# Latent attention: value products of four heads issued as one quad on four column groups, with eight exponential buffers

## The chip, the cores and the metric

One core of a Trainium2 chip runs the whole program. Times are microseconds on the device. The kernel before took 2137.08 us, the median of three runs (2136.1 to 2139.33). Less is better.

## The reference, cut to what matters

The program computes six stages on a state of 16 elements of 256 rows by 128: two mixtures of experts with a gated attention unit between them, a second kind of mixture (gate/up, "swiglu"), a latent attention, and that second mixture again. Only the latent attention changes. For each of the 16 elements (`b`) it computes, with 16 heads of 8 columns:

```python
ct_q = x @ Wd_q_w + Wd_q_b
query = heads(ct_q @ Wu_q_w + Wu_q_b) + heads(_rope(ct_q @ Wq_r_w + Wq_r_b, cos, sin))
ct_kv = x @ Wd_kv_w + Wd_kv_b
key = heads(ct_kv @ Wu_k_w + Wu_k_b) + heads(_rope(x @ Wk_r_w + Wk_r_b, cos, sin))
value = heads(ct_kv @ Wu_v_w + Wu_v_b)
attn = softmax(einsum('bhqd,bhkd->bhqk', query, key) / scale)
out = einsum('bhqk,bhkd->bhqd', attn, value)          # back to (b, s, d_model)
x = x + (out @ Wo_w + Wo_b)
```

All of it is float32. The softmax's maximum of each row is found first (the "search"), then folded into the scores as two extra rows, and its sum comes out of the value product as one more column of ones.

## The kernel before, in words

Each engine has its own program, written out by hand, and the engines wait for each other by counting semaphores (`p.at_ex` counts exponentials, `p.at_av` value products, and so on). The order is a software pipeline over elements: while element b goes through its 16 heads, TensorE also does the end of element b-1 and the preparation of b+1 and b+2 between the heads.

TensorE's order is `at_pe_element` (L1687 on). In step h it issues the scores of head h (`at_scores_pe`, L1644: two matmuls of 26 rows by 128 columns over 256 columns, into bank 3 or 4 in turn, waiting for the exponential of head h-2), and the value products of head h-2 (`at_values_pe`, L1656). Other work hangs on certain steps: 1 the turn of the second half of the maxima's rows (L1606); 2 the turn of the output of b-1 (L1668); 3 the turn of the keys of b+1 (L1582, waits for VectorE's and ScalarE's parts); 4 the turn of x of b+2 (L145); 5 the turn of the queries (L1582); 6 the turn back of the output (L1675); 7 the latent product (L1555); 8 the output product (L1683); 9 the rotary keys (L1563); 7 to 14 two searches each (L1631: 24 rows); 12 the first half of the maxima's rows; 17 the projections of b+2 (L1573, waits for all 16 maxima). Steps 16 and 17 have no scores, only values.

A value product of one head is two matmuls (one for each half of the keys) of 128 rows by 32 columns over 256 columns, accumulated in bank 7. The 32 columns of head a are those from 32 x (a mod 4), so four consecutive heads use four different groups of columns of the array. In the trace each such float32 matmul is two records, so a head is four.

ScalarE's order is `at_act_element` (L1813 on): the exponential of head h (L1818) from bank 3 or 4 into one of four buffers (head mod 4), after the value product of head h-4 has been done; between them copies out of the banks: maxima rows (L1798), parts (L1776), keys and queries (L1781), x, latent, rotary keys (L1756, L1762, L1768), the outputs of heads 0 to 7 after head 9 and of 8 to 15 at the end (L1805).

VectorE's order is `at_dve_element` (L1957 on): the split parts of b+1 (L1897, L1901), the normalised x of b+2 (L136), the norm of the output of b-1 (L1937, L1941), bias and statistics (L1947, L100, L104), two maxima (L1910), the addition to X (L1954), fourteen maxima with two small row writes after the eighth and the sixteenth (L1919, L1921), and the projections' biases and rotation (L1875 to L1888). A search goes into one of three banks, and TensorE waits for the maximum of the search three before it.

The stage's tiles lie in tensors that earlier stages are done with. `g2b` and `be2b` hold the norm weights of the first kind of mixture and are read only there.

Of the kernel before, what the change touches and what calls it, by code (L numbers as in the profile page):

```python
# [13 lines left out]
ACT = mybir.ActivationFunctionType  # L14
AX = mybir.AxisListType

P = 128
B, S, D = 16, 256, 128
# [69 lines left out]
def flat(ap):  # L88
    return ap.rearrange("p a b -> p (a b)")
# [1104 lines left out]
NB2 = 2  # L1194
# [338 lines left out]
NH, HD = 16, 8  # L1533
HR = 32
HQ = P // HR
NHQ = NH // HQ
NPROD = 3 * HD
LATENT = 64
ATT_SCALE = 1.0 / float(np.sqrt(NH + 2 * LATENT))
SEARCH_BANKS = (1, 2, 5)  # L1540
HALF_BANKS = (6, 0)
OUT_BANKS = (5, 6)
LAG = 2
# [23 lines left out]
def at_project_pe(pe, p, b):  # L1567

    pe.wait_ge(p.at_mx.sem, p.at_mx.at(NH * b))
    for n in range(2):  # L1570
        r = slice(n * LATENT, (n + 1) * LATENT)
        for t in range(NB2):
# [48 lines left out]
def at_search_pe(pe, p, b, par, f):  # L1621
# [6 lines left out]
    for n in range(2):  # L1628
        h = pair % HQ + HQ * (2 * (pair // HQ) + n)
        r = head_rows(h, NPROD)  # L1630
        ins = pe.matmul(p.bk[SEARCH_BANKS[f % 3]][:, n * S:(n + 1) * S], p.at_qT[r, h // HQ, t * P:(t + 1) * P],  # L1631
# [4 lines left out]
def at_scores_pe(pe, p, b, par, h):  # L1636
# [3 lines left out]
    if h >= 2:  # L1640
        pe.wait_ge(p.at_ex.sem, p.at_ex.at(NH * b + h - 1))
    r = head_rows(h, NPROD + 2)
    for t in range(NB2):
# [2 lines left out]
    ins.then_inc(p.at_s2.sem, 1)  # L1646


def at_values_pe(pe, p, b, par, a):

    pe.wait_ge(p.at_ex.sem, p.at_ex.at(NH * b + a + 1))
    if a % 8 == 0:
        pe.wait_ge(p.at_op.sem, p.at_op.at(2 * b + a // 8))
    o = p.bk[7][HR * (a % HQ):HR * (a % HQ + 1), (a // HQ) % 2 * S:((a // HQ) % 2 + 1) * S]
    for t in range(NB2):
        ins = pe.matmul(o, p.at_v[:, par, t, a, :], p.at_e[:, a % 4, t * S:(t + 1) * S],  # L1656
                        start=(t == 0), stop=(t == NB2 - 1))
    ins.then_inc(p.at_av.sem, 1)


# [26 lines left out]
def at_pe_element(pe, p, b, par, behind=True, ahead=2):  # L1687


    for h in range(NH + LAG):  # L1690
        if h < NH:
            at_scores_pe(pe, p, b, par, h)
        if h >= LAG:
            at_values_pe(pe, p, b, par, h - LAG)
        if h == 1:
            pe.wait_ge(p.at_kr.sem, p.at_kr.at(b + min(ahead, 1) + 1))
            at_maxima_rows_pe(pe, p, b, 1)
        if behind:
            if h == 2:
                at_out_turn_pe(pe, p, b - 1)  # L1700
            elif h == 6:
                at_out_back_pe(pe, p, b - 1)
            elif h == 8:
                at_out_pe(pe, p, b - 1)
        if ahead >= 1:
            if h == 3:
                at_keys_pe(pe, p, b + 1)
            elif h == 5:
                at_queries_pe(pe, p, b + 1)
            if 7 <= h < NH - 1:  # L1710
                for f in range(2 * (h - 7), 2 * (h - 6)):
                    at_search_pe(pe, p, b + 1, 1 - par, f)
            if h == 12:
                at_maxima_rows_pe(pe, p, b + 1, 0)
        if ahead >= 2:
            if h == 4:
                pe.wait_ge(p.at_q2.sem, p.at_q2.at(2 * b + 2))
                at_x_pe(pe, p, b + 2)
            elif h == 7:
                at_latent_pe(pe, p, b + 2)  # L1720
            elif h == 9:
                at_kr_pe(pe, p, b + 2)
            elif h == NH + LAG - 1:
                at_project_pe(pe, p, b + 2)
# [76 lines left out]

def at_heads_out_act(act, p, b, half):

    act.wait_ge(p.at_av.sem, p.at_av.at(NH * b + 8 * half + 8))
    act.activation(flat(p.at_o[:, 2 * half:2 * half + 2, :]), p.bk[7][:], ACT.Copy).then_inc(p.at_op.sem, 1)  # L1805


# [5 lines left out]
def at_act_element(act, p, b, par, behind=True, ahead=2):  # L1813
    for h in range(NH):
        act.wait_ge(p.at_s2.sem, p.at_s2.at(NH * b + h + 1))
        if h >= 4:
            act.wait_ge(p.at_av.sem, p.at_av.at(NH * b + h - 3))
        act.activation(p.at_e[:, h % 4, :], p.bk[3 + h % 2][:], ACT.Exp, scale=ATT_SCALE).then_inc(p.at_ex.sem, 1)  # L1818
        if h == 1:
            at_maxima_rows_act(act, p, b, 1)  # L1820
        if h == 7 + LAG:
            at_heads_out_act(act, p, b, 0)
        if ahead >= 1:
            if h == 2:
                at_parts_act(act, p, b + 1)
            elif h == 4:
                at_keys_act(act, p, b + 1, 1 - par)
            elif h == 6:
                at_queries_act(act, p, b + 1)
            elif h == 12:  # L1830
                at_maxima_rows_act(act, p, b + 1, 0)
        if ahead >= 2:
            if h == 5:
                at_x_act(act, p, b + 2)
            elif h == 8:
                at_latent_act(act, p, b + 2)
            elif h == 10:
                at_kr_act(act, p, b + 2)
        if behind and h == 7:
            at_out_act(act, p, b - 1)  # L1840
    at_heads_out_act(act, p, b, 1)
# [73 lines left out]
def at_maxima_rows_dve(dve, p, b, half):  # L1915

    h = slice(half * NH // 2, (half + 1) * NH // 2)
    dve.wait_ge(p.at_mx.sem, p.at_mx.at(NH * b + (half + 1) * NH // 2))
    dve.tensor_copy(p.at_sk_r[:, 0, :, h, NPROD], p.at_m[:, :, h]).then_inc(p.at_nm.sem, 1)  # L1919
    dve.wait_ge(p.at_nm.sem, p.at_nm.at(4 * b + 2 * half + 1))  # L1920
    dve.tensor_tensor(p.at_sk_r[:, 0, :, h, NPROD + 1], p.at_m[:, :, h], p.at_sk[:, 0, :, h, NPROD], ALU.subtract)\  # L1921
       .then_inc(p.at_nm.sem, 1)
# [78 lines left out]
def at_pool(pool, p):  # L2001
# [3 lines left out]
    pool.wait_ge(p.at_init.sem, p.at_init.at(2))  # L2005
    pool.memset(p.at_sk[:, 1, :, :, NPROD:NPROD + 2], 1.0).then_inc(p.at_init.sem, 1)
    for par in range(2):
# [5 lines left out]
def at_weights_dve(dve, p):  # L2013
# [25 lines left out]
    "mla": dict(ln_free=B, ln_stat=2 * NT, ln_rs=2 * B, xt=B, at_xc=B, at_ctp=B, at_ct=B, at_krp=B, at_kr=B,  # L2039
                at_prp=2 * B, at_q=NS1 * B, at_hc=2 * B, at_ktp=2 * B, at_kt=2 * B, at_qtp=2 * B, at_qt=2 * B,  # L2040
                at_s1=NH * B, at_mx=NH * B, at_nm=4 * B, at_q2p=2 * B, at_q2=2 * B, at_s2=NH * B, at_ex=NH * B,
                at_av=NH * B, at_op=2 * B, at_otp=B, at_on=4 * B, at_tp=B, at_ot=B, at_wp=B, at_x1=B, at_x=B,
                at_init=5),
    "swiglu": dict(_PREP, **_COMB, gt_rows=NCH * NG, up_rows=NCH * NG, silu_d=NCH * NG, hid_d=NCH * NG, exp_d=E1 * NG,
                   exp_add=TG * E1 * NG, rtg=NG, rt3=2 * NG),
# [62 lines left out]
def work_space(t):  # L2108

    at = Space(t.tables)  # L2110
    w = {n: at.take(P, cols) for n, cols in TABLES.items()}
    at = Space(t.sb_)
    w.update(r=at.take(P, TG, F), rT=at.take(P, 2, F), y=at.take(P, 2, TG, D))
    at = Space(t.sc)
    w.update(yo=at.take(P, 2, TG, D), slots=at.take(P, 2, TG, D), t_ge=at.take(P, SLOT_TILES, E),
             t_skip=at.take(P, SLOT_TILES, E), c_move=at.take(P, TOP * NT, E), xT=flat(t.xf[:]), be1s=t.wd[:, 0:F], w1_last=t.sb_[0:1, :],
             c2s=t.sc[:].rearrange("p (e f) -> p e f", f=F)[:, :, 0:D],
             ga_taken=(flat(t.xf[:]), t.sel[:].rearrange("p k t e -> p (k t e)")))
    at = Space(t.sb_, 2 * W)
    w.update(sw_taken=(at.take(P, W), at.take(P, W)))  # L2120

    w.update(hT=Space(t.sc).take(P, HRING, W), sg=Space(t.sb_).take(P, 2, W))

    at = Space(t.sb_)
    w.update(ga_xa=at.take(P, S), ga_q=at.take(NQ, S), ga_h=at.take(NQ, 2, S), ga_r1=at.take(NQ, 2, S),
             ga_r2=at.take(NQ, 2, S), ga_r=at.take(NQ, 2, 2, S), ga_k=at.take(P, P), ga_s=at.take(NQ, H))
    at = Space(t.sc)
    w.update(ga_v=at.take(P, 2, NB2, 2 * H), ga_a1=at.take(P, NB2, P), ga_a=at.take(P, NB2, P),
             ga_g=at.take(P, NB2, H), ga_t=at.take(P, 4 * P))
    at = Space(t.sa, 2 * ROWS)  # L2130
    w.update(ga_yy=at.take(P, NB2, D), ga_z=at.take(P, NB2, D), ga_st=at.take(P, NB2, 6), ga_mv=at.take(P, NB2, 2),
             ga_ve=at.take(P, NB2), ga_sc=at.take(P, NB2))

    at = Space(t.w2c)
    w.update(at_w=at.take(P, 2 * P), at_last=at.take(P, 2 * P), at_u=at.take(P, 2 * D), at_b=at.take(P, 4 * D),
             at_wo=at.take(P, D), at_bo=at.take(P, D), at_cos=at.take(P, S), at_sin=at.take(P, 2, S // 2))
    at = Space(t.w1h)
    w.update(at_qT=at.take(P, NHQ, S), at_qT2=at.take(P, NHQ, S))
    at = Space(t.sa)
    w.update(at_e=at.take(P, 4, NB2 * S), at_sk=at.take(P, 2, NB2, NH, HR))  # L2140
    w.update(at_sk_r=w["at_sk"].bitcast(F32R))
    at = Space(t.sb_)
    w.update(at_v=at.take(P, 2, NB2, NH, HR), at_xa=at.take(P, S), at_c=at.take(P, S), at_r=at.take(P, 2, NB2, D),
             at_s=at.take(P, 2, NB2, D), at_t1=at.take(P, 2, NB2, D))
    at = Space(t.sc)
    w.update(at_t2=at.take(P, 2, NB2, D), at_o=at.take(P, NHQ, S), at_n=at.take(P, NB2, D), at_t=at.take(P, S),
             at_m=at.take(P, NB2, NH), at_rc=at.take(P, NB2, NH))
    w.update(at_kT=[x[:].rearrange("p a (b s) -> p (a b) s", s=S) for x in (t.xh, t.xl)])
    return w
# [271 lines left out]
```

## Time and profile before

| what | value |
|---|---|
| median of the runs | 2137.08 us |
| span of the profiled execution | 2134.5 us (the runs' median is 2.6 us above it) |
| TensorE busy | 1807.3 us, 85% |
| VectorE busy | 1259.6 us, 59% |
| ScalarE busy | 688.6 us, 32% |
| GpSimd busy | 585.9 us, 27% |
| latent attention | some 500 of the 2134.5 us, 16 elements |

Busy times are of the profiled execution. An engine's busy share says nothing by itself about what sets the end; the chain of waits and the stretches of a single stage do. The granted clock is a fraction of TensorE's full 2.4 GHz: 1.00 is 2.4, 0.50 is 1.2.

### The profile page before, as it was taken

To read this page: it belongs to the slowest core of one execution; us is meant where nothing else is said; L and a number is where in the kernel's file an instruction comes from. 1 tells how busy PE (TensorE), PEld (TensorE's weight loads), DVE (VectorE), ACT (ScalarE), POOL (GpSimd) and SP (SyncE) were. 2 spreads that over 40 slices of the span, in tenths; PEclk is the share of its full clock that TensorE was granted. 3 is DMA by queue.
4 is the path that set the end of the run, shared out by engine and by line. 5 is a ranking of instruction groups with operands and counts; after the bars stand their busy time and mean duration, and the time that the engine had idled before them with its cause. 6 is when DMAs were issued, how large, how long until landed. Compare 5 with 4: busy or idle time off the path is not lost.

```text
span 2134.5 us, 38192 instructions
## 1 busy us (share of the span) xinstructions
PE 1807.3 (85%) x10652; PEld 1360.9 (64%) x10653; DVE 1259.6 (59%) x4249; ACT 688.6 (32%) x1279; POOL 585.9 (27%) x946
## 2 busy tenths in 40 slices
PE   3759993888834599479999979999999998999998
PEld 2548991444433499468888855555555555988997
DVE  2546884666544588656656645655655652656654
ACT  0115550222200255223223214444444443223222
POOL 2653775555247366631221010000000000000000
PEclk9658996787755699789999979999999999999999
DMA  5111212000001122200000000000000000000001
GB/s 196 39 45 50 61 49 92 21 18 19 5 20 43 57 58 60 57 23 11 14 15 10 1 1 1 1 1 0 0 0 0 0 0 1 1 0 0 0 1 40
DMA packets 61674, 54.01 MB, mean 25 GB/s; under 512 B 8467, under 2 KB 54932, under 8 KB 61077
## 3 DMA queue, kind: packets, MB, share of 16 engines
q1 hardware_dynamic: 51958, 34.11, 5.2%
q0 software_dynamic: 8192, 16.79, 2.6%
q10 hardware_dynamic: 1440, 2.10, 0.3%
q8 instruction: 39, 0.64, 0.1%
q14 instruction: 45, 0.37, 0.1%
HBM read 31.48 MB, written 21.50 MB: 25 GB/s over the span
## 4 chain that ended last, share of the span: by engine, by line
PE 70%; issue 10%; DVE 9%; POOL 6%; DMA 2%; SPq 1%; ACT 1%; POOLq 1%; DVEq 1%; ACTq 0%
PE bk L1007 14%; PE bk L1656 10%; PE bk L582 6%; PE bk L990 5%; PE bk L992 5%; PE bk L991 5%; PE bk L1644 3%; PE bk L575 3%; PE bk L1631 2%; PE bk L1582 2%; PE bk L564 2%; PE bk L566 2%; PE bk L565 2%; DMA sb_X<-x 1%; POOL sb_xf L455 1%
## 5 line engine op out<-in xcount | busy, mean ns | idle before, releaser
L1007 PEld LDWEIGHTS bk<-sb_wd,sb_sc 128*128 128x128 f32 (+1 forms) x2688 | 332.9, 191 | 24.8 <-DVE sb_X L1106 3.6
L1007 PE MATMUL bk<-sb_wd,sb_sc 128*128 128x128 f32 (+1 forms) x2688 | 336.9, 275 | 0.9 <-issue 0.8
L1092 DVE TENSOR_TENSOR sb_sc<-sb_sb_,bk 128x512 f32<-128x512 f32 x224 | 152.2, 684 | 240.5 <-PE bk L992 190.4
L112 POOL TENSOR_TENSOR sb_ln_ve<-sb_ln_mv,sb_eps 128x2 f32<-128x2 f32 (+1 forms) x48 | 9.4, 195 | 1010.2 <-DVE sb_ln_mv L104 1010.2
L1046 ACT ACTIVATE sb_sb_<-bk 128x512 f32<-128x512 f32 x224 | 133.9, 598 | 450.8 <-PE bk L992 448.4
L1910 DVE TENSOR_REDUCE sb_sc<-bk 128x2 f32<-128x512 f32 x256 | 164.6, 687 | 156.2 <-PE bk L1631 152.1
L1656 PE MATMUL bk<-sb_sa,sb_sb_ 128*32 128x256 f32 x1024 | 247.4, 385 | 0.7 <-ACT sb_sc L1805 0.7
L1818 ACT ACTIVATE sb_sa<-bk 128x512 f32<-128x512 f32 x256 | 151.1, 597 | 182.8 <-PE bk L1644 182.8
L1106 DVE SCALAR_TENSOR_TENSOR sb_X<-bk,sb_gate,sb_X 128x128 f32 (+1 forms) x576 | 161.4, 342 | 4.2 <-PE bk L1007 1.8
L582 PE MATMUL bk<-sb_w2c,sb_sb_ 128*128 x1152 | 152.1, 275 | 0.0
L368 POOL DMA_INDIRECT xs<-sb_xn,sb_send_row x128 | 128.8, 1006 | 83.6 <-DVE sb_send_row L357 48.3
L1656 PEld LDWEIGHTS bk<-sb_sa,sb_sb_ 128*32 128x32 f32 x1024 | 86.4, 109 | 84.6 <-ACT sb_sa L1818 2.8
L582 PEld LDWEIGHTS bk<-sb_w2c,sb_sb_ 128*128 128x128 f32 x1152 | 140.0, 192 | 0.2
L632 ACT ACTIVATE sb_sb_<-bk 128x512 f32<-128x512 f32 x144 | 86.0, 597 | 121.0 <-PE bk L566 120.9
L669 DVE BATCH_NORM_STATS2 sb_st<-sb_sb_ 128x6 f32<-128x512 f32 x144 | 92.9, 683 | 45.1 <-ACT sb_sb_ L632 42.9
L990 PE MATMUL bk<-sb_xh,sb_wgh 128*128 128x512 f32 x224 | 107.7, 481 | 1.1 <-issue 1.1
L992 PE MATMUL bk<-sb_xl,sb_wuh 128*128 128x512 f32 x224 | 88.9, 397 | 0.7 <-issue 0.7
L991 PE MATMUL bk<-sb_xh,sb_wgl 128*128 128x512 f32 x224 | 88.9, 397 | 0.6 <-issue 0.6
L992 PE MATMUL bk<-sb_xl,sb_wgh 128*128 128x512 f32 x224 | 89.2, 398 | 0.1
L638 ACT ACTIVATE sb_sb_<-bk 128x512 f32<-128x512 f32 x144 | 85.9, 597 | 10.4 <-PE bk L575 10.3
L990 PE MATMUL bk<-sb_xh,sb_wuh 128*128 128x512 f32 x224 | 89.1, 398 | 0.1
L991 PE MATMUL bk<-sb_xh,sb_wul 128*128 128x512 f32 x224 | 88.4, 394 | 0.3 <-issue 0.3
(279 smaller groups left out, 3418.7 us busy)
## 6 DMA issues: line engine op xcount, KB each, us to landing
sb_sc<-xs SPq DMA_DIRECT2D x144, 64.0 KB, 1.8
ys<-sb_sc SPq DMA_DIRECT2D x36, 256.0 KB, 2.3
xs<-sb_xn,sb_send_row POOLq DMA_INDIRECT x128
out<-sb_X SPq DMA_DIRECT2D x1, 2048.0 KB, 8.7
sb_sa<-w SPq DMA_DIRECT2D x1, 1792.0 KB, 13.3
sb_sc<-w SPq DMA_DIRECT2D x1, 1792.0 KB, 17.8
sb_sa<-w_gu SPq DMA_DIRECT2D x1, 1760.0 KB
xs<-sb_zeros SPq DMA_DIRECT2D x24, 64.0 KB, 17.8
```

What stands on the lines that cost most here:

```text
L368: pool.indirect_dma_start(p.xs, bass.IndirectOffsetOnAxis(ap=p.send_row[:, par, k, j:j + 1], axis=0), xn[:, par, j, :], None).then_inc(p.s ...
L582: ins = pe.matmul(p.bk[4 + par][:, j * P:(j + 1) * P], p.rT[:, j % 2, c * P:(c + 1) * P], p.w2c[:, bass.ds((e * FC + c) * D, D)], start=(c ...
L990: pe.matmul(bank[0:m, :], w_h[:, rows], p.xh[:, par, :], start=True, stop=False)
L991: pe.matmul(bank[0:m, :], w_l[:, rows], p.xh[:, par, :], start=False, stop=False)
L992: pe.matmul(bank[0:m, :], w_h[:, rows], p.xl[:, par, :], start=False, stop=True).then_inc(done.sem, 1)
L1007: ins = pe.matmul(bank[:, j * P:(j + 1) * P], p.hT[0:m, c % HRING, j * P:(j + 1) * P], p.wd[0:m, q * D:(q + 1) * D], start=(c == FIRST[e] ...
L1046: act.activation(p.sg[0:m, c % 2, :], p.bk[c % 2][0:m, :], ACT.Silu).then_inc(p.silu_d.sem, 1)
L1092: dve.tensor_tensor(p.hT[0:m, c % HRING, :], p.sg[0:m, c % 2, :], p.bk[2 + c % 2][0:m, :], ALU.mult)\
L1106: dve.scalar_tensor_tensor(out=x, in0=p.bk[DBANK[e % 3]][:, j * P:(j + 1) * P], scalar=p.gate1[:, par, j, e:e + 1], in1=x, op0=ALU.mult, o ...
L1656: ins = pe.matmul(o, p.at_v[:, par, t, a, :], p.at_e[:, a % 4, t * S:(t + 1) * S], start=(t == 0), stop=(t == NB2 - 1))
L1818: act.activation(p.at_e[:, h % 4, :], p.bk[3 + h % 2][:], ACT.Exp, scale=ATT_SCALE).then_inc(p.at_ex.sem, 1)
L1910: dve.tensor_reduce(p.at_m[:, t, :].rearrange("p (q r) -> p q r", r=HQ)[:, q:q + 2, pair % HQ], p.bk[SEARCH_BANKS[f % 3]][:].rearrange("p ...
```

## The change

Three things change in the latent attention. The value products are issued for four heads at once (`quad`): for each half of the keys the four heads in turn, each on its own column group, and one semaphore count for a quad in place of four; a quad is issued in steps 5, 9, 13 and 17, two steps after its last head's scores. The exponentials have eight buffers instead of four; four lie where they were, two in `g2b` and two in `be2b`, and exponential h waits for the quad that held head h-8. ScalarE's copy of heads 0 to 7 moves from after exponential 9 to after exponential 10.

```diff
+NQUAD = NH // HQ
+ERING = 8
...
-def at_values_pe(pe, p, b, par, a):
-
-    pe.wait_ge(p.at_ex.sem, p.at_ex.at(NH * b + a + 1))
-    if a % 8 == 0:
-        pe.wait_ge(p.at_op.sem, p.at_op.at(2 * b + a // 8))
-    o = p.bk[7][HR * (a % HQ):HR * (a % HQ + 1), (a // HQ) % 2 * S:((a // HQ) % 2 + 1) * S]
+def at_values_pe(pe, p, b, par, quad):
+
+    pe.wait_ge(p.at_ex.sem, p.at_ex.at(NH * b + HQ * (quad + 1)))
+    if quad % 2 == 0:
+        pe.wait_ge(p.at_op.sem, p.at_op.at(2 * b + quad // 2))
     for t in range(NB2):
-        ins = pe.matmul(o, p.at_v[:, par, t, a, :], p.at_e[:, a % 4, t * S:(t + 1) * S],
-                        start=(t == 0), stop=(t == NB2 - 1))
+        for r in range(HQ):
+            a = HQ * quad + r
+            o = p.bk[7][HR * r:HR * (r + 1), quad % 2 * S:(quad % 2 + 1) * S]
+            ins = pe.matmul(o, p.at_v[:, par, t, a, :], p.at_e[a % ERING][:, t * S:(t + 1) * S],
+                            start=(t == 0), stop=(t == NB2 - 1))
     ins.then_inc(p.at_av.sem, 1)
...
-        if h >= LAG:
-            at_values_pe(pe, p, b, par, h - LAG)
+        if h >= HQ + LAG - 1 and (h - LAG) % HQ == HQ - 1:
+            at_values_pe(pe, p, b, par, (h - LAG) // HQ)
...
-    act.wait_ge(p.at_av.sem, p.at_av.at(NH * b + 8 * half + 8))
+    act.wait_ge(p.at_av.sem, p.at_av.at(NQUAD * b + 2 * half + 2))
...
-        if h >= 4:
-            act.wait_ge(p.at_av.sem, p.at_av.at(NH * b + h - 3))
-        act.activation(p.at_e[:, h % 4, :], p.bk[3 + h % 2][:], ACT.Exp, scale=ATT_SCALE).then_inc(p.at_ex.sem, 1)
+        if h >= ERING:
+            act.wait_ge(p.at_av.sem, p.at_av.at(NQUAD * b + (h - ERING) // HQ + 1))
+        act.activation(p.at_e[h % ERING], p.bk[3 + h % 2][:], ACT.Exp, scale=ATT_SCALE).then_inc(p.at_ex.sem, 1)
...
-        if h == 7 + LAG:
+        if h == 8 + LAG:
             at_heads_out_act(act, p, b, 0)
...
-    w.update(at_e=at.take(P, 4, NB2 * S), at_sk=at.take(P, 2, NB2, NH, HR))
+    heads = [at.take(P, NB2 * S) for _ in range(4)]
+    w.update(at_sk=at.take(P, 2, NB2, NH, HR))
+    for bank in (Space(t.g2b), Space(t.be2b)):
+        heads += [bank.take(P, NB2 * S) for _ in range(2)]
+    w.update(at_e=heads)
```

## Rows read from the trace of the kernel before

**Rows 1.** The page: span, busy time by engine, chain by line, one group.
```profile
span 2134.5 us, 38192 instructions
PE 1807.3 (85%) x10652; PEld 1360.9 (64%) x10653; DVE 1259.6 (59%) x4249; ACT 688.6 (32%) x1279; POOL 585.9 (27%) x946
PE bk L1007 14%; PE bk L1656 10%; PE bk L582 6%; PE bk L990 5%; PE bk L992 5%; PE bk L991 5%; PE bk L1644 3%; PE bk L575 3%; PE bk L1631 2%; PE bk L1582 2%; PE bk L564 2%; PE bk L566 2%; PE bk L565 2%; DMA sb_X<-x 1%; POOL sb_xf L455 1%
```

**Rows 2.** Busy time by stretches: the stage, then two of its elements.
```profile
core 0: us, PE busy (x) PEld busy (x) DVE busy (x) ACT busy (x) POOL busy (x), PEclk, DMA share, GB/s
1290.00:1793.00 503.00, 486.76 (x2828) 269.28 (x2828) 284.11 (x653) 239.35 (x469) 11.58 (x26) 1.00 0.00 0
1448.46:1480.29 31.83, 31.09 (x185) 17.31 (x183) 19.02 (x46) 15.17 (x30) 0.89 (x2) 1.00 0.00 0
1480.29:1512.23 31.94, 31.09 (x185) 17.30 (x183) 19.01 (x46) 15.17 (x30) 0.89 (x2) 1.00 0.00 0
```

**Rows 3.** Groups of one element, 1480.29 to 1512.23: busy, mean, idle before.
```profile
L1656 PE MATMUL bk<-sb_sa,sb_sb_ 128*32 128x256 f32 x64 | 15.5, 385 | 0.0
L1910 DVE TENSOR_REDUCE sb_sc<-bk 128x2 f32<-128x512 f32 x16 | 10.3, 687 | 9.6 <-PE bk L1631 9.4
```

**Rows 4.** Timeline of TensorE from an element's first scores: start, us, idle before.
```profile
1511.79 0.50 PE L1644 MATMUL bk<-sb_w1h,sb_xl 26*128 26x256 f32 x4
1512.22 0.66 PE L1606 MATMUL bk<-sb_tables,sb_sa 128*128 128x128 f32 x4
1512.98 0.50 PE L1644 MATMUL bk<-sb_w1h,sb_xl 26*128 26x256 f32 x2
1513.41 1.05 PE L1656 MATMUL bk<-sb_sa,sb_sb_ 128*32 128x256 f32 x4
1514.39 1.09 PE L1668 MATMUL bk<-sb_tables,sb_sc 128*128 128x128 f32 x8
...
1517.54 1.09 PE L1582 MATMUL bk<-sb_tables,sb_sa 128*128 128x128 f32 x8 [0.64 <-DVE sb_sa L1901]
...
1519.97 0.44 PE L145 MATMUL bk<-sb_tables,sb_xn 128*128 128x128 f32 x2
1520.34 0.50 PE L1644 MATMUL bk<-sb_w1h,sb_xl 26*128 26x256 f32 x2
```

**Rows 5.** Timeline at the end of an element, matmuls and exponential.
```profile
1508.98 1.81 PE L1656 MATMUL bk<-sb_sa,sb_sb_ 128*32 128x256 f32 x12
1509.09 0.60 ACT L1818 ACTIVATE sb_sa<-bk 128x512 f32<-128x512 f32 x1 [0.99 <-PE bk L1644]
1510.72 1.14 PE L1573 MATMUL bk<-sb_w2c,sb_sb_ 64*128 64x256 f32 x8
```

**Rows 6.** Timeline of VectorE and ScalarE ahead of the keys, and after.
```profile
1511.88 1.42 DVE L1875 TENSOR_TENSOR sb_sb_<-bk,sb_w2c 128x256 f32<-128x256 f32 x4 [1.31 <-PE bk L1573]
1516.65 0.76 DVE L1901 TENSOR_TENSOR sb_sa<-sb_sb_,sb_sa 128x256 fp32r<-128x256 f32 x2
1519.59 1.08 ACT L1781 ACTIVATE sb_xh<-bk 128x512 fp32r<-128x512 f32 x2
```

**Rows 7.** The chain, in the opening: start, us, what.
```profile
1281.94 4.79 DVE sb_sc L1910 x8
```

**Rows 8.** Busy time by stretches, gated unit and opening, TensorE and clock.
```profile
380.00:600.00 220.00, 177.69 (x603) 93.58 (x602) 131.54 (x406) 46.73 (x102) 105.59 (x185) 0.75 0.06 15
423.40:430.20 6.80, 6.01 (x16) 3.07 (x17) 3.81 (x14) 2.01 (x5) 4.88 (x7) 0.50 0.15 39
430.20:437.00 6.80, 6.48 (x26) 3.29 (x24) 5.97 (x18) 1.20 (x2) 1.71 (x7) 1.00 0.00 0
437.00:443.80 6.80, 5.07 (x16) 2.61 (x15) 3.20 (x12) 1.63 (x4) 5.61 (x8) 0.50 0.14 39
1274.00:1287.00 13.00, 10.50 (x39) 8.10 (x40) 10.24 (x20) 0.77 (x2) 0.00 (x0) 0.50 0.00 1
1290.40:1300.90 10.50, 9.49 (x52) 5.52 (x52) 5.18 (x14) 7.06 (x14) 0.89 (x2) 1.00 0.00 2
```

**Rows 9.** Opening: searches as a group (1274 to 1287), then the timeline.
```profile
L1631 PE MATMUL bk<-sb_xh,sb_w1h 24*128 24x256 f32 x32 | 9.0, 494 | 1.0 <-DVE sb_sc L1910 1.0
1286.78 2.09 PE L1573 MATMUL bk<-sb_w2c,sb_sb_ 64*128 64x256 f32 x8 [1.00 <-DVE sb_sc L1910]
1288.79 1.11 PE L1606 MATMUL bk<-sb_tables,sb_sa 128*128 128x128 f32 x4
```

More of the change, by code:

```diff
@@ L2041 @@
                 at_s1=NH * B, at_mx=NH * B, at_nm=4 * B, at_q2p=2 * B, at_q2=2 * B, at_s2=NH * B, at_ex=NH * B,
-                at_av=NH * B, at_op=2 * B, at_otp=B, at_on=4 * B, at_tp=B, at_ot=B, at_wp=B, at_x1=B, at_x=B,
+                at_av=NQUAD * B, at_op=2 * B, at_otp=B, at_on=4 * B, at_tp=B, at_ot=B, at_wp=B, at_x1=B, at_x=B,
                 at_init=5),
```

## The prediction

> **What bounds the kernel now.** I read the page first: TensorE is the busiest engine and the lines of the attention's products of values (L1656) and scores lead among its lines [rows 1]. The busy time by stretches then shows that the attention proper is a stage of its own from 1290 to 1793 us, that its elements repeat every 31.9 us, and that TensorE is busy 31.1 us of each while VectorE has 19.0 and ScalarE 15.2 [rows 2]. So TensorE is the bound, at the full granted clock (1.00, 2.4 GHz). The groups of one element split its work: 64 matmuls of L1656 have the largest share, 15.5 us [rows 3]. The timeline gives what they really hold: a head (4 matmuls) starts at 1513.41 and the next operation at 1514.39, 0.98 us [rows 4]. The last three heads of an element come back to back and are different: 12 matmuls from 1508.98, and the next operation (the projections, L1573) at 1510.72, so 1.74 us for three heads in place of 2.94 [rows 5]. Per element the values hold 13 x 0.98 + 1.74 = 14.5 us of TensorE. Its only real stall is 0.64 us before the turn of the keys (L1582), which waits for VectorE [rows 4].
>
> **Part 1: four heads together.** The four heads of a quad write four different sets of 32 output columns. The three that stand together now, 13 to 15, cost 1.74 us: heads 13 and 14 fit in about the time of one, 15 began later because its exponential was late (ScalarE's L1818 in that stretch runs to 1509.69, and head 15 adds the second 0.98 almost whole) [rows 5]. If four ready heads overlap as two do, a quad holds TensorE for 0.98 us plus some 0.04, say 1.02. The other end is four at 0.98, 3.9 us (no overlap of a third and fourth); two at a time is a little more than three heads cost now, 1.85. I take 1.02, the nearest to the row that shows ready heads overlapping. Taken out of TensorE: 14.5 - 4 x 1.02 = 10.4 us an element. Were TensorE still the only bound, that would be 16 x 10.4 = 166 us. It won't be: next are the chains.
>
> The Trainium skill, "TensorE: Matmul & The Clock Gate", Part 3 (Measured speedup vs the span model), gives 2.38 times for three column tiles, not 3. No row here has three ready at once. By it a quad would be an estimated 4 x 0.98 / 3.2 = 1.2 us, and the sum below would be at most 4 x 0.2 x 16 = 13 us later.
>
> **Part 2: what is late next.** I walk one new element, T = 0 at its first scores, all at full clock, with the old order but values only at steps 5, 9, 13 and 17.
> - Scores 0 and 1 go together, 0.43; turn of the maxima (L1606) 0.58; scores 2 wait for exponential 0 until 1.19 as now (1512.98 against 1511.79); out turn (L1668) 1.02, scores 3: TensorE is free at 3.07 [rows 4]. Two heads of values that filled 1.96 us here are gone.
> - The keys wait for VectorE's rotation: L1875 starts at 1511.88 and L1901 ends at 1517.41, the turn starts at 1517.54, T + 5.75 [rows 4, 6]. Nothing in the change makes this earlier. The 0.64 us stall becomes 5.75 - 3.07 = 2.7 us.
> - Keys 1.02, scores 4, turn of x 0.37, scores 5, quad 0 (1.02), queries 1.02, scores 6, turn back 0.37, scores 7: to 11.3. ScalarE has to copy the turned queries behind exponential 6 (from about 10.6, then 1.08 for the two copies as with the keys, L1781): the first search goes at 12.2, a second stall of 0.9 us [rows 4, 6].
> - Now VectorE's 16 maxima. In the opening, where nothing else is in their way, 8 of them take 4.79 us, 0.60 each [rows 7], which makes 9.7 us; the two small row writes after the eighth add 0.4, the addition to X 0.4. The searches are pulled by VectorE through three banks, and TensorE's own work between them (latent, keys' rotary part, out product, about 0.64 each, quads 1 and 2, maxima turn) leaves VectorE some 2 us without input: 12.75 to 25.5. So the last third of the element is no longer TensorE's at all.
> - Exponential 15 ends at about 25.3; quad 3 stands before the projections, to 26.4; projections (L1573) 1.07: the next element begins at T + 27.45.
> So an element at full clock is 27.45 instead of 31.9: 4.4 x 16 = 71 us, a little more in the last element, where 1.41 us a head (0.43 + 0.98) can fall to the scores' own round of about 0.6. Of TensorE's 10.4 us, 6 become stalls.
>
> **Part 3: eight buffers, the counters, ScalarE's copy.** Exponentials 4 to 7 go to two other tensors. Nothing reads those in this stage; 0. Exponential 8 waits for quad 0 (T + 9) and starts at about 13.8; 12 waits for quad 1 (T + 15.6), starts at 21.6: neither wait ends last. Below nothing: no gain there either, TensorE's waits for exponentials come from scores. The copy of heads 0 to 7 goes behind exponential 10 instead of 9; quad 2 waits for it, at 18.3 against 21.5, 0; with that cover gone it would cost its own 0.6 us. No DMA is issued or moved.
>
> **Part 4: the granted clock.** This is the term that decides. What TensorE does when its clock is at half (0.50, 1.2 GHz) stands in two places. In the earlier gated unit the clock changes back and forth: 423.4 to 430.2 and 437.0 to 443.8 at 0.50, between them 1.00, 0.75 over 380 to 600, though TensorE is busy 81% there; it fell at 437.0 after a stretch in which it was busy 6.48 of 6.80 us [rows 8]. And ahead of the first element, 1274 to 1287, it is busy 81% mostly with searches of 24 rows, at 0.50 throughout, and the full clock comes at 1290.4, after the projections (64 rows) and the turn of the maxima (128 rows) [rows 8, 9]. Busy share alone does not hold the clock. The new element has both traits: 2.7 us of idleness ahead of the keys, and a long search part of 24 and 26 rows with three of four value stretches removed. So I expect falls in nearly every element.
> The price: the projections take 2.01 us at half (1286.78 to 1288.79) against 1.07 (1510.72 to 1511.79) [rows 5, 9]. An element wholly at half would be TensorE's again: 31.9 - 0.6 - 14.5 + 4.1 = 20.9 us of its work, times about 1.95, near 41 us. A share s of the time at half then takes 1 - 27.45/41 = 0.33 of that time: period = 27.45 / (1 - 0.33 s). With s = 0: 27.45. With s = 1/2, as in the gated unit: 32.9. Break-even with 31.9: s = 0.42. The attention's elements are denser than that unit's, with 128-row turns and quads in the middle; I take s = 1/3, some 10 us of each element: 27.45 / 0.89 = 30.9. That gives 16 x (31.9 - 30.9) = 16 us, and 3 for the last element: 19.
>
> The sum is made on the profiled execution: its span of 2134.5 us becomes 2115.5; the median of the runs is 2.6 above that span, so 2137 - 19 = **2118 us**.
>
> **Rivals.**
> - *The clock holds.* s near 0 to 0.15: 27.5 to 28.9 an element, 48 to 74 us won, about 2067. For it: the present elements have a 0.64 us stall in each and not one fall in 490 us [rows 2]. Against: the rows of the opening searches.
> - *The clock is at half so much that the change loses.* One mechanism: the value products are what now keeps the clock up; four at once in 1 us do not count as four, and the search part from T + 17 on cannot hold it. From s = 0.42 on it is slower; at s = 0.5, 32.9 an element, 16 us slower, 2153. For it: the opening searches and the gated unit [rows 8]. Against: quads 1 and 2 stand in that part.
> - *The column groups do not run four wide.* At 1.85 a quad: 4 x 0.83 = 3.3 us more an element where TensorE is the bound, of which the new stalls hide little: 30.8 at full clock, and with the falls 33: 2115 to 2160. For it: no row has more than two at once. Against: the pair in rows 5 shows no loss at all. Without any overlap nothing is saved and the later values add stalls: over 2160.
>
> **How the numbers follow.** Forecast case (s about 0.2 to 0.4; 2104 to 2134) 0.45; clock holds 0.23; clock lost 0.22; groups not wide 0.10. From these: range 2060 to 2150, which takes in most of the first rival and the milder half of the second. No change within 0.2% (about what a measurement of this kernel can tell, 4 us) 0.09, from the edges of the forecast and of the last two; faster 0.70; slower 0.21.
>
> **What would show it.** Quads: 16 matmuls of L1656 in about 1.0 us. The turn of the keys with an idle time of 2.5 to 3 us ahead of it, released by L1901. VectorE's maxima the largest part of the chain in the last third of an element. The granted clock of the stage between 0.75 and 0.9 instead of 1.00, with falls after the keys' stall. The prediction is wrong if the stage keeps 1.00 (then elements near 27.5), if its mean is under 0.75, or if a quad takes 1.8 us or more.

## The result and the profile after

The changed kernel takes 2226.54 us, the median of four runs (2223.94 to 2232.08), against 2138.2 us for the kernel before on the same chip (four runs): ratio 1.0417, 95% interval 1.0403 to 1.0432. It is 88 us slower, where 2118 us, 19 us faster, was forecast.

The page of the changed kernel, span and busy time, and its clock line (tenths of full speed in 40 slices); [rows 1] answer to it:

```profile
span 2230.3 us, 38140 instructions
PE 1848.0 (83%) x10652; PEld 1417.8 (64%) x10653; DVE 1256.4 (56%) x4249; ACT 685.1 (31%) x1279; POOL 586.5 (26%) x946
PEclk9559995777655999699999855565555575999999
```

The same instructions (10652 matmul records in both), and the long run of mostly 5 and 6 near the end of the clock line (24th to 34th slice) is the latent attention. The busy time of the changed kernel by stretches, with the columns of [rows 2]: the stage, one element wholly at half clock, and the shortest element:

```profile
1290.00:1888.00 598.00, 526.79 (x2832) 326.94 (x2832) 281.76 (x656) 235.86 (x469) 11.58 (x26) 0.57 0.00 0
1556.60:1596.10 39.50, 36.56 (x187) 22.94 (x183) 18.82 (x44) 15.04 (x30) 0.89 (x2) 0.50 0.00 0
1481.00:1517.00 36.00, 30.19 (x188) 18.78 (x184) 18.82 (x44) 14.86 (x30) 0.89 (x2) 0.69 0.00 0
```

The stage has grown from 503 to 598 us, which is nearly all of the 96 us between the two spans. VectorE and ScalarE do what they did (18.8 and 15.0 us an element against 19.0 and 15.2). The granted clock went from 1.00 to 0.57. Fourteen elements, from projections to projections, take 536.5 us (1287.8 to 1824.3), 38.3 each, against 31.9. Five of them are wholly at half clock; the others have a mean of 0.54 to 0.69.

The timeline of TensorE at the head of the element wholly at half clock, with the columns of [rows 4]:

```profile
1556.58 2.09 PE L1575 MATMUL bk<-sb_w2c,sb_sb_ 64*128 64x256 f32 x8
1558.60 0.80 PE L1646 MATMUL bk<-sb_w1h,sb_xl 26*128 26x256 f32 x4
1559.32 1.11 PE L1608 MATMUL bk<-sb_tables,sb_sa 128*128 128x128 f32 x4
...
1564.34 1.97 PE L1584 MATMUL bk<-sb_tables,sb_sa 128*128 128x128 f32 x8 [0.56 <-DVE sb_sa L1905]
...
1568.30 1.94 PE L1660 MATMUL bk<-sb_sa,sb_sb_ 128*32 128x256 f32 x16
1570.17 1.97 PE L1584 MATMUL bk<-sb_tables,sb_sa 128*128 128x128 f32 x8
```

A quad, 16 matmul records, holds TensorE 1.87 us here at half clock. The turn of the keys starts 5.74 us after the first scores (1564.34 - 1558.60), as it did before, but the idle time ahead of it is only 0.56 us: at half clock the rest of TensorE's work fills the hole. In this element TensorE is the bound again, busy 36.56 of 39.50 us, at half speed.

The shortest element shows the other kind of head. Its clock was full when it came to the keys; first its scores and its keys, then, in the busy time by stretches, the head up to the keys and 5 us soon after the turn has begun:

```profile
1482.63 0.51 PE L1646 MATMUL bk<-sb_w1h,sb_xl 26*128 26x256 f32 x4
1488.39 1.40 PE L1584 MATMUL bk<-sb_tables,sb_sa 128*128 128x128 f32 x8 [2.62 <-DVE sb_sa L1905]
```
```profile
1482.63:1488.39 5.76, 3.05 (x23) 2.17 (x21) 5.49 (x13) 2.97 (x7) 0.00 (x0) 1.00 0.00 0
1490.00:1495.00 5.00, 5.00 (x29) 2.95 (x29) 0.55 (x4) 2.34 (x5) 0.89 (x2) 0.50 0.00 0
```

Here the stall ahead of the keys is 2.62 us, as forecast (2.7), and the clock falls right behind it. Six of the thirteen elements behind the first are of this kind, with a stall of 2.1 to 2.7 us; in each the clock is at half by 2 us after the start of the turn. So the clock comes back now and then, and each time it falls at the keys.

### The profile page after: what moved, and what is told of

It reads as the page before. It is cut to its first block, busy times and chain, and to the rows that moved or that the text cites. A ratio compares the mean times of both kernels' runs of the same rounds, so it can differ in the third digit from the quotient of the medians.

```text
span 2230.3 us, 38140 instructions
## 1 busy us (share of the span) xinstructions
PE 1848.0 (83%) x10652; PEld 1417.8 (64%) x10653; DVE 1256.4 (56%) x4249; ACT 685.1 (31%) x1279; POOL 586.5 (26%) x946
## 4 chain that ended last, share of the span: by engine, by line
PE 68%; DVE 11%; issue 10%; POOL 5%; ACT 2%; DMA 1%; SPq 1%; POOLq 1%; DVEq 1%; ACTq 0%
PE bk L1007 14%; PE bk L582 5%; PE bk L1660 5%; PE bk L990 5%; PE bk L992 5%; PE bk L991 5%; PE bk L1633 3%; PE bk L1646 3%; PE bk L575 3%; PE bk L1584 3%; DVE sb_sc L1914 2%; PE bk L564 2%; PE bk L566 2%; PE bk L565 2%; PE bk L1575 1%
## 5 line engine op out<-in xcount | busy, mean ns | idle before, releaser
L1822 ACT ACTIVATE sb_sa<-bk 128x512 f32<-128x512 f32 x128 | 74.9, 598 | 126.6 <-PE bk L1646 125.4
L575 PE MATMUL bk<-sb_tables,sb_sb_ 128*128 128x128 f32 x576 | 87.8, 275 | 0.0
L1646 PE MATMUL bk<-sb_w1h,sb_xl 26*128 26x256 f32 x256 | 83.6, 460 | 1.7 <-ACT sb_sa L1822 1.5
```

Of the source, the lines that this page charges most:

```text
L575: ins = pe.transpose(p.bk[2 + j % 2][:, c * P:(c + 1) * P], p.r[:, j, c * P:(c + 1) * P], p.ident)
L1646: ins = pe.matmul(p.bk[3 + h % 2][:, t * S:(t + 1) * S], p.at_kT[par][r, h // HQ, t * P:(t + 1) * P], p.at_qT2[r, h // HQ, :], start=True, ...
```

## The experiments

Seven of the eleven kernels ask why the clock fell, four how to do the change without that. The kernel before took 2128.74, 2128.99 and 2129.4 us beside them, not 2138.2, so each is given as a ratio too. The changed kernel was not run again beside them; by its ratio it would stand at an estimated 1.0417 x 2129 = 2218 there.

**The value products over 32 rows (values_32_rows).** In the kernel before:

```diff
+    pe.matmul(o[:, 0:8], p.at_v[:, par, 0, a, :], p.at_e[:, a % 4, 0:8], start=True, stop=True)
     for t in range(NB2):
-        ins = pe.matmul(o, p.at_v[:, par, t, a, :], p.at_e[:, a % 4, t * S:(t + 1) * S],
+        ins = pe.matmul(o, p.at_v[0:32, par, t, a, :], p.at_e[0:32, a % 4, t * S:(t + 1) * S],
```

> The kernel before with each value product over 32 of its 128 rows (three quarters of the keys are left out of the sum), and one 8-column matmul of 128 rows ahead of each head to carry the wait. As many long matmuls in the same order, TensorE as busy. Theory (value products of 128 rows hold the clock, busy time as such does not): the stage falls to a granted clock of 0.5 to 0.7 and the kernel is slower than 2220. Rival (only idleness costs the clock): clock 1.00, within 20 us of 2137.

Measured: 2593.01 us, ratio 1.218 (1.2156 to 1.2204). One element of it in the busy time by stretches:

```profile
1396.80:1458.30 61.50, 61.50 (x215) 31.77 (x214) 19.19 (x44) 15.58 (x30) 0.89 (x2) 0.50 0.00 1
```

TensorE is busy for the whole 61.5 us, and the clock is at 0.50 for all of it. There are four value records a head as before, in the same places, but of 32 rows (and two short ones of 128 rows and 8 columns, 4.4 us an element). So being busy is not enough to get the full clock; with 128-row value products the same order had it. Two groups of the element from 1396.76 to 1458.32, the values and the turns of keys and queries:

```profile
L1657 PE MATMUL bk<-sb_sa,sb_sb_ 32*32 32x256 f32 x65 | 31.2, 629 | 0.0
L1582 PE MATMUL bk<-sb_tables,sb_sa 128*128 128x128 f32 x16 | 3.9, 428 | 0.0
```

The turns of 128 rows are all still there, 9.5 us of the 61.5 in their five lines, and they did not bring the clock up.

**Part 3 of the change alone (ring8_alone).** Eight buffers and ScalarE's copy moved, values one head at a time:

```diff
-        if h >= 4:
-            act.wait_ge(p.at_av.sem, p.at_av.at(NH * b + h - 3))
-        act.activation(p.at_e[:, h % 4, :], ...
+        if h >= 8:
+            act.wait_ge(p.at_av.sem, p.at_av.at(NH * b + h - 7))
+        act.activation(p.at_e[h % 8], ...
...
-        if h == 7 + LAG:
+        if h == 8 + LAG:
             at_heads_out_act(act, p, b, 0)
```

> The kernel before with only the eight exponential buffers and the moved copy of heads 0 to 7; values stay one head at a time. Theory (the loss comes from the granted clock, which the long single value products held up): 2137 within 3 us, stage clock 1.00. Rival (the new places of the buffers or the moved copy cost time): a part of the 88 us stays here, over 2150.

Measured: 2189.58 us, ratio 1.0278 (1.0261 to 1.0295). My expectation was wrong: the ratio means 60 us more than the kernel before, and the rival seemed to have it. The timeline of one element shows where:

```profile
1335.25 1.02 PE L1656 MATMUL bk<-sb_sa,sb_sb_ 128*32 128x256 f32 x4 [1.27 <-ACT sb_sc L1805]
```

Head 8's values now wait 1.27 us for the moved copy in step 10; with quads nothing is issued there. Two elements of the same run, in the busy time by stretches:

```profile
1424.10:1457.30 33.20, 31.08 (x183) 17.32 (x182) 19.02 (x44) 15.07 (x30) 0.89 (x2) 1.00 0.00 0
1457.40:1496.60 39.20, 37.19 (x185) 19.77 (x184) 19.09 (x44) 15.17 (x30) 0.89 (x2) 0.83 0.00 0
```

The wait itself costs 1.3 us (33.2 against 31.9), and some elements keep the full clock in spite of it. Where the clock falls behind it, as in the second, the element costs 7.3. To part the two halves, the copy was put back:

```diff
-        if h == 8 + LAG:
+        if h == 7 + LAG:
```

> Eight exponential buffers with values one head at a time, and ScalarE's copy of heads 0 to 7 left where it was, after exponential 9. It splits the run before (ring8_alone, 61 us slower). Theory (the moved copy makes head 8 wait in step 10, about 1.3 us of idleness in the part of the element that has least 128-row work, and the clock falls there): as the kernel before within 4 us, clock as before. Rival (the new places of the buffers cost it): still over 2170.

Measured: 2129.09 against 2128.99 us, ratio 0.9999 (0.9990 to 1.0009). The buffers are free, and 1.3 us more of idleness in step 10 is enough for the kernel before to lose its clock in part of its elements.

**Useless work in the quads kernel (quads_keys_filled, quads_all_filled).** The first adds, to the changed kernel,

```diff
 def at_keys_pe(pe, p, b):
+    pe.wait_ge(p.at_q.sem, p.at_q.at(NS1 * b + 4))
+    for _ in range(10):
+        pe.matmul(p.bk[1][:, 0:P], p.ident, p.ident, start=True, stop=True)
```

> The changed kernel with ten matmuls of 128 rows by 128 columns (2.1 us of TensorE at full clock, results overwritten) in the stall ahead of the turn of the keys, nothing else. Rival that the prediction named (the stall ahead of the keys starts the falls and the rest follows from it): clock near 1.00, elements near 28, 2065 to 2090. Theory (the whole element, above all the search part, is too thin in 128-row work once four heads run as one): a partial gain only, about 2170, clock 0.7 to 0.8.

and the second, besides, in `at_scores_pe` after its waits:

```diff
+    for _ in range(2 if h >= 6 else 0):
+        pe.matmul(p.bk[3 + h % 2][:, 0:P], p.ident, p.ident, start=True, stop=True)
```

> The same with, besides, two such matmuls (0.43 us at full clock) ahead of the scores of heads 6 to 15: 4.3 us of useless work more in each element, where TensorE is not the bound at full clock. Theory: the clock is back to 0.95 or more and the kernel is faster for the added work: 2110 to 2150. Rival (waits and the order lose the time, not the clock): slower than the changed kernel, 2230 to 2290.

Measured: 2175.05 us, ratio 1.0217 (1.0187 to 1.0246), for the first; 2129.32 us, ratio 1.0014 (0.9983 to 1.0045), for the second. More work, faster: 43 us less than the 2218 estimated for the changed kernel with one fill, 89 less with both. The second is the least steady kernel here (2115.09 to 2145.67 in eight runs; the profiled one took 2117.83). A typical element of the first, then of the second:

```profile
1489.70:1524.30 34.60, 32.23 (x206) 21.95 (x202) 18.82 (x44) 14.99 (x30) 0.89 (x2) 0.70 0.00 0
```
```profile
1465.50:1496.50 31.00, 29.45 (x246) 21.56 (x242) 18.91 (x44) 14.91 (x30) 0.90 (x2) 1.00 0.00 0
```

Filling the hole ahead of the keys gives half of it back, so that stall takes part but isn't the whole. Where the clock falls instead shows in another element of the first, one that comes to the keys at full clock: from the head to 1438, past the keys and the first search, then the search part.

```profile
1425.00:1438.00 13.00, 11.97 (x89) 8.63 (x88) 7.88 (x23) 7.75 (x18) 0.89 (x2) 1.00 0.00 0
1439.00:1449.00 10.00, 8.98 (x54) 5.88 (x51) 6.77 (x13) 3.44 (x7) 0.00 (x0) 0.50 0.00 0
```

So the search part is too thin as well. The useless matmuls of both fills are 60 records an element and keep TensorE busy 9.1 us of it in the trace (2.5 ahead of the keys, 6.6 ahead of the scores), more than the 6.4 that I had reckoned with; at full clock the element needs 31.0 us with them. Its timeline also shows the quad at full clock:

```profile
1474.64 1.07 PE L1665 MATMUL bk<-sb_sa,sb_sb_ 128*32 128x256 f32 x16
1475.64 1.09 PE L1584 MATMUL bk<-sb_tables,sb_sa 128*128 128x128 f32 x8
```

The quad starts at 1474.64 and the next operation at 1475.64: 1.00 us for four heads, where one took 0.98.

**Two heads at a time (pairs).** `quad` becomes a group of two, issued in steps 3, 5, ..., 17; the copy stays after exponential 9.

```diff
-        if h >= HQ + LAG - 1 and (h - LAG) % HQ == HQ - 1:
-            at_values_pe(pe, p, b, par, (h - LAG) // HQ)
+        if h >= GRP + LAG - 1 and (h - LAG) % GRP == GRP - 1:      # GRP = 2
+            at_values_pe(pe, p, b, par, (h - LAG) // GRP)
```

> Values of two heads at once instead of four, eight buffers, the copy after exponential 9. Theory (column groups that run together count once for the clock, and the value work must stay long enough): values hold TensorE some 8 us an element instead of 4 (quads) or 14.5 (before), the clock falls less: elements of 28 to 30 us, clock of the stage 0.85 to 0.95, kernel 2085 to 2110. Rival (grouping as such loses the clock because values come late and in lumps): over 2129, the kernel before on this chip.

Measured: 2096.53 us, ratio 0.9824 (0.9789 to 0.9860). That is inside the range, but the elements are longer than expected: most take 30.6 to 30.8 us. One (1367.9 to 1395.1) keeps the full clock and takes 27.2. Twelve of them:

```profile
1307.00:1678.00 371.00, 337.94 (x2186) 206.16 (x2184) 225.60 (x528) 178.97 (x360) 10.70 (x24) 0.85 0.00 0
```

> Pairs, and six useless matmuls of 128 by 128 (1.3 us at full clock) in the stall ahead of the keys. Theory: full clock nearly throughout, 2055 to 2080, faster than pairs by 20 to 40 us though it does more work. Rival: no faster than pairs.

Measured, with the fill of six matmuls ahead of the keys: 2061.34 us, ratio 0.9686 (0.9670 to 0.9702), 35 us faster than pairs. An element:

```profile
1419.40:1446.60 27.20, 25.95 (x196) 16.50 (x194) 18.80 (x44) 14.86 (x30) 0.89 (x2) 1.00 0.00 0
```

**The amount or the places (quads_two_groups).** In the changed kernel:

```diff
-    for t in range(NB2):
-        for r in range(HQ):
-            o = p.bk[7][HR * r:HR * (r + 1), ...
+    for t, r in ((0, 0), (0, 1), (1, 0), (1, 1), (0, 2), (0, 3), (1, 2), (1, 3)):
+            o = p.bk[7][HR * (r % 2):HR * (r % 2 + 1), ...
```

> The changed kernel with each quad in its old place, but its third and fourth head written over the first and second (the outputs of half the heads are lost), so that two column groups run at a time and a quad takes some 1.85 us at full clock, as two pairs one behind the other. It parts two things that pairs change at once: how much value work there is (8 us an element in both), and where it stands. If the amount alone decides, this runs like the pairs, 2085 to 2110. If the places count as much (four lumps leave the stretches between them thin, and each lump delays scores and searches), it stays near the quads, 2200 to 2240. I expect the second.

Measured: 2256.9 us, ratio 1.0600 (1.0571 to 1.0630), a little beyond what I expected. An element:

```profile
1474.40:1515.40 41.00, 35.69 (x185) 20.58 (x183) 18.80 (x44) 14.75 (x30) 0.89 (x2) 0.71 0.00 0
```

The value work is about that of the pairs, the clock is 0.71 instead of 0.85, and the element takes 41.0 us instead of 30.7. So not only how much 128-row work there is counts, but that it stands spread over the element.

Against the quads the same kernel is the closest look at the amount: the same multiplications in the same steps, only two column groups at a time in place of four. Over 1300 to 1700 us the clock is 0.73, where the quads have 0.55. The time is longer all the same, since each quad takes more of TensorE.

**Projections ahead of the last group.** In step 17 `at_project_pe` goes ahead of the last value group, and VectorE waits for that group before it writes the next values:

```diff
+        if ahead >= 2 and h == NH + LAG - 1:
+            at_project_pe(pe, p, b + 2)
         if h >= GRP + LAG - 1 and (h - LAG) % GRP == GRP - 1:
...
+        if m == 3 and waited is not None:
+            dve.wait_ge(p.at_av.sem, p.at_av.at(NQUAD * (waited + 1)))
```

> Quads with the projections ahead of the last quad. The chain is 1 us shorter in each element, and 1 us of 128-row work stands where the stall ahead of the keys was. If quads lose only by the clock, this helps by far more than the 16 us of the chain: 2130 to 2160, clock of the stage 0.65 to 0.8. If it were the chain, 2200 to 2210.

Measured with quads: 2203.52 us, ratio 1.0350 (1.0329 to 1.0370). I had expected 2130 to 2160; it gains some 15 us, what the chain gives, and its clock stayed at 0.55:

```profile
1533.20:1570.70 37.50, 34.72 (x182) 22.00 (x182) 18.84 (x45) 15.11 (x31) 0.89 (x2) 0.55 0.00 0
```

> Pairs, and in step 17 the projections are issued ahead of the last pair, so that VectorE's rotation starts 1 us earlier and the last pair fills the time of the stall ahead of the keys (VectorE waits for the element's values before it writes the next values tile). Theory: one us less of chain and one less of idleness, elements of 27.5 to 28.5, clock over 0.95, kernel 2045 to 2070. Rival (the clock is not helped by where the pair stands): the gain over pairs is at most 16 us.

Measured with pairs: 2063.86 us, ratio 0.9691 (0.9674 to 0.9707), 33 us faster than pairs, twice what the chain explains: here the clock rises from 0.85 to 0.94. Thirteen elements, 28.0 us each, then one at full clock:

```profile
1308.00:1672.00 364.00, 339.93 (x2366) 204.93 (x2364) 243.75 (x566) 191.87 (x390) 10.70 (x24) 0.94 0.00 0
1423.00:1449.60 26.60, 24.73 (x182) 15.08 (x182) 18.82 (x44) 14.75 (x30) 0.89 (x2) 1.00 0.00 0
```

The last kernel adds two useless matmuls ahead of the keys and one ahead of scores 12.

> Pairs with the projections first, two useless matmuls ahead of the keys and one ahead of scores 12 in each element: the clock still falls in some elements of the run without them (0.93 in the middle of the stage). Theory: over 0.97, 2045 to 2060, some 5 to 15 us faster than 2064. Rival: no change, the fills cost what they give.

Measured: **2048.69 us, ratio 0.9624 (0.9608 to 0.9640)**, against 2129.4 before: 81 us faster than the kernel before, the best of all. The stage's middle:

```profile
1304.00:1656.00 352.00, 341.88 (x2446) 209.79 (x2444) 243.76 (x566) 191.77 (x390) 10.69 (x24) 0.98 0.00 0
```

## Why the prediction was wrong

**The quads (Part 1): right.** 16 records in 1.00 us at full clock, 1.02 taken. The Trainium skill, "TensorE: Matmul & The Clock Gate", Part 3 (Measured speedup vs the span model), has 2.38 times for three column tiles. Here four tiles of float32 gave 4 x 0.98 / 1.00 = 3.9 times, and the 1.2 us estimated from that page was too high. The rival that the groups do not run four wide falls.

**What is late next (Part 2): right in its first third, not seen as a whole.** The keys start at T + 5.74 to 5.94, 5.75 was said, and where the clock is full the stall ahead of them is 2.62 us for 2.7. The full period of 27.45 us could not be seen, since no steady element of the quads ran at full clock without fills. The nearest are the pairs at full clock, 27.2 with or without the fill and 26.6 with the projections first: the order of size is right.

**Eight buffers, counters and the copy (Part 3): right for the change.** The buffers cost 0 (ratio 0.9999). The copy's new place is harmless only because the quads issue nothing in step 10; with single heads it costs 1.3 us an element by itself and, with the clock that it loses, 60 us in all.

**The clock (Part 4): the step that failed.** The mechanism held: the clock falls behind the stall ahead of the keys and in the search part. Its price held roughly. With the measured mean clock of 0.57 the share at half is s = (1 - 0.57) / 0.5 = 0.86, and 27.45 / (1 - 0.33 x 0.86) = 38.3 us. That this is exactly the measured period is partly luck: an element wholly at half took 39.5 us, where 41 was said, and the one at 0.69 (s = 0.62) took 36.0, where the formula gives 34.5. What was wrong is "I take s = 1/3", a term that no row gave; the runs showed s = 0.86. I took it on the ground that the elements are "denser than that unit's, with 128-row turns and quads in the middle". The runs show that four column groups at once did not keep the clock as four one after the other had: the same multiplications, done in 4 us instead of 14.5 and in four lumps, left 0.57, and the same order with value products of 32 rows left 0.50 at 100% busy, with all the 128-row turns in place. The rival "the value products are what now keeps the clock up; four at once in 1 us do not count as four" fits what happened, and I gave it 0.22 and ended it at s = 0.5. By the prediction's own formula s = 1 would have been 41 us an element, and no case had a price for s above a half. Over the stage the clock comes back for only a seventh of the time: in an element at half the hole ahead of the keys closes (0.56 us) and TensorE is busy 36.56 of 39.50 us, but with thin work; where the clock does come back, the next stall of 2.6 us is followed by a fall.

The size of the miss has one more cause. The rows had a unit at half for half of the time (s = 1/2) and the opening searches at half throughout (s = 1), and I went below both. The 490 us without a fall, which I counted for the rival that the clock holds, belonged to the very work the change removes. A slip beside it: the forecast case names 2104 to 2134 for s of 0.2 to 0.4, where the prediction's formula gives some 2094 to 2130; the result lies outside either.

**What would show it.** Of the four signs named, the quad came as said; the idle time ahead of the keys was 2.1 to 2.7 us, released by L1905 and followed by a fall, where the clock was full, and 0.56 to 0.75 us where it was at half, since TensorE comes later there; VectorE's maxima hold 11.6% of the chain in the last third of an element (1578.0 to 1596.1), less than L1660 and L1633 of TensorE with 31% and 25%; and the clock of the stage was under the 0.75 named as the mark of a wrong prediction.

What stays open: which activity exactly the chip counts. That the rows of the value products matter is shown by values_32_rows, and that the same products hold the clock better two groups at a time than four by quads_two_groups. That concurrent column groups count exactly once was only argued. No kernel had a fill of few rows, so the fills do not part the rows from the end of the idleness; and whether the turns count at all was not measured by itself. The quads' own period at full clock was not seen either.

## What to carry to other kernels

Packing matmuls into column groups takes away TensorE's time and, with it, the work that holds its clock: before such a change ask, for each stretch of a period, what 128-row work is left in it and whether the clock was ever full in a stage as thin. Prefer the smaller group spread evenly (pairs here: 0.98) to the larger in lumps (quads: 1.04), and move a block of full-height matmuls into the longest stall; if a stall stays, useless full-height matmuls in it can be worth tens of microseconds in all (six of them in each element of the pairs, 1.6 us busy, gave 35). A small new stall in a kernel near that edge can cost several times its own length (three times here), so read the granted clock of each period before its waits.

## What the runs showed of the hardware

- A granted clock of 0.50 for a whole stage with TensorE busy 100% (61.5 of 61.5 us, matmuls of 24 to 32 rows for the most part).
- Four column groups with float32 operands run side by side almost without loss: 16 records in 1.00 us, 4 in 0.98.
- In the changed kernel the granted clock falls from 1.00 to 0.50 within 2 us of the end of an idle stretch of 2.62 us; with that stretch filled it stays at 1.00 past the turn of the keys (1429.84) to 1438 and falls in the search part.
- Idle time of 1.27 us more in each element of 31.9 us took the stage's clock from 1.00 to 0.90 and cost 60 us, three times the idle time itself.
- Adding 9.1 us of useless 128-row matmuls to elements of 38.3 us on average made most of them 31.0.
